# A selective-scan layer on one Trainium2 core: TensorE's half sums of y in front of the fills, GpSimd's first dt*u product of a chunk one place later

## The reference

```python
def step(h, inp):                       # K=4 directions, 192 channels, 16 states
    ul, dl, Bl, Cl = inp
    dA = jnp.exp(dl[..., None] * A)
    h = dA * h + (dl * ul)[..., None] * Bl[:, :, None, :]
    y = jnp.einsum('bkdn,bkn->bkd', h, Cl)
    return (h, y)
```

## Time and profile before

| | |
|---|---|
| Times of three runs | 11091.9, 11092.8, 11114.3 us (median 11092.8) |
| The profiled execution | 11114.1 us, its span 11112.4 us |
| Busy over the span | VectorE 9404 us, TensorE 9796, GpSimd 9035, ScalarE 8690 |
| GpSimd's weighings (L1004) | 3072 of 2383 ns, 7204 us; 358 us idle before them, 278 of it for line 714 |
| VectorE's scans (L779) | 3072 of 2273 to 2333 ns; 518 us idle before them |
| TensorE's granted clock | 0.954 of full speed, mean |

### The profile page before, as it was taken

One profiled execution on the slowest core, in us unless ns is written; L12 is line 12 of the kernel. 1 busy time (PEld: TensorE's weight loads), 2 busy tenths in 40 slices (PEclk: granted clock), 3 DMA queues, 4 the chain that ended last, 5 costly groups with the idle time before them and its releaser, 6 DMA issues. The chain is left out here.

```text
span 11112.4 us, 345302 instructions
## 1 busy us (share of the span) xinstructions
PE 9796.2 (88%) x142892; PEld 6546.6 (59%) x142892; DVE 9404.3 (85%) x5727; ACT 8689.8 (78%) x15618; POOL 9035.1 (81%) x3978
## 2 busy tenths in 40 slices
PE   8978888888888888888888888888888889799999
PEld 5645555555555555555555555555555555588888
DVE  7869999998999999989999998999999999555554
ACT  3468888888888888888888888888888888345453
POOL 1169999999999999999999999999999999534330
PEclk9989999999999999999999999999999999899999
DMA  3356666666666666666666666666666666322220
GB/s 103 108 153 160 167 174 171 161 167 170 174 161 167 177 167 162 168 173 167 159 167 175 166 161 166 175 170 162 172 177 164 159 171 163 84 75 64 70 70 13
DMA packets 547249, 1647.95 MB, mean 148 GB/s; under 512 B 148562, under 2 KB 149362, under 8 KB 542872
## 3 DMA queue, kind: packets, MB, share of 16 engines
q1 hardware_dynamic: 484248, 1416.10, 50.0%
q10 hardware_dynamic: 61440, 209.76, 6.1%
HBM read 1251.98 MB, written 373.29 MB: 146 GB/s over the span
## 5 line engine op out<-in xcount | busy, mean ns | idle before, releaser
L1004 POOL TENSOR_TENSOR HC<-H,crep 128x1024 f32<-128x1024 f32 x3072 | 7203.9, 2383 | 358.0 <-PE psum L714 277.7
L779 DVE TENSOR_TENSOR_SCAN H<-E,car,psum 128x1024 f32<-128x1024 f32 x2304 | 5271.4, 2333 | 344.8 <-PE psum L691 111.2
L880 ACT ACTIVATE E<-dlr,am 128x1024 f32<-128x1024 f32 x3072 | 3497.2, 1145 | 917.2 <-DVE H L779 868.6
L714 PE MATMUL psum<-HC,sely 128*32 128x512 f32 x12288 | 2307.0, 635 | 83.4 <-POOL HC L1004 65.2
L779 DVE TENSOR_TENSOR_SCAN H<-E,psum 128x1024 f32<-128x1024 f32 x768 | 1713.5, 2273 | 173.4 <-PE psum L691 78.1
L691 PE MATMUL psum<-diagp,dluT 128*32 128x128 f32 x49152 | 1630.3, 276 | 256.0 <-DVE H L779 240.8
L691 PE MATMUL psum<-diag,dluT 128*32 128x128 f32 x49152 | 1692.7, 280 | 145.7 <-issue 121.1
L691 PEld LDWEIGHTS psum<-diagp,dluT 128*32 128x32 f32 x49152 | 1387.0, 111 | 681.0 <-DVE H L779 488.9
L691 PEld LDWEIGHTS psum<-diag,dluT 128*32 128x32 f32 x49152 | 1448.2, 112 | 496.0 <-issue 377.3
L862 ACT ACTIVATE sdl<-dluT,blt 128x192 f32<-128x192 f32 x4096 | 1507.5, 444 | 0.0
L680 PE MATMUL psum<-idn,sdl 128*128 128x128 f32 x6144 | 953.2, 305 | 566.2 <-DVE H L779 566.2
(11 more groups left out here) (143 smaller groups left out, 10428.2 us busy)
## 6 DMA issues: line engine op xcount, KB each, us to landing
dlr<-scr_dl SPq DMA_DIRECT2D x3072, 128.0 KB, 4.2
dur<-scr_dlu SPq DMA_DIRECT2D x3072, 128.0 KB, 3.3
crep<-scr_bc SPq DMA_DIRECT2D x512, 256.0 KB, 6.4
crep<-scr_bc SPq DMA_DIRECT2D x1024, 128.0 KB, 3.0
scr_dlu<-dlu SPq DMA_DIRECT2D x256, 384.0 KB, 3.1
scr_yk<-yt ACTq DMA_DIRECT2D x256, 384.0 KB, 3.0
scr_dl<-dlt ACTq DMA_DIRECT2D x128, 384.0 KB, 4.4
scr_dl<-yt ACTq DMA_DIRECT2D x128, 384.0 KB, 4.2
```

What stands on the lines that cost most here:

```text
L714: r = e.matmul(yps[32 * j:32 * j + 32, cols], sely[:], HC[:, (3 * i + j) % NHC, cols], start=g == 0 and k != 0 and not second(m), stop=g = ...
L779: e.tensor_tensor_scan(H[:, un % NH, ::step], decay[:, ::step], drive[:, ::step], init, ALU.mult, ALU.add).then_inc(scan_done)
L880: e.activation(E[:, un % NE, :], dlr[:, slot(m, j), :], ACT.Exp, scale=am[:, ae:ae + 1]).then_inc(exp_done)
L1004: e.tensor_tensor(HC[:, un % NHC, :], H[:, un % NH, :], crep[:, g, :], ALU.mult).then_inc(hc_done)
```

## The change

In TensorE's loop the half sum now comes before `fill(un + 2)`, save at x = 5, where the fill stays first. GpSimd's `delta` of an even step comes at x = 9, behind weighing 8, and no longer at x = 8, behind weighing 7.

```diff
         for un in range(NUNIT + 12):
             n, x = divmod(un, 12)
-            fill(un + FILL_AHEAD)
+            if x == 5:
+                fill(un + FILL_AHEAD)
             if un >= 5 and (un - 5) % 3 < 2 and (un - 5) // 3 < NG * NSTEP:
                 sum_y((un - 5) // 3, (un - 5) % 3)
+            if x != 5:
+                fill(un + FILL_AHEAD)
...
             if n % 2 == 0:
-                if x == 8 and n + 2 < NSTEP:
+                if x == 9 and n + 2 < NSTEP:
                     delta(n + 2)
```

## The result

The changed kernel is slower: median 11138.1 us of six runs (11127.0 to 11150.6), against 11102.7 us for the kernel before in six runs, ratio **1.0031, 95% interval 1.0020 to 1.0042**, +35 us. The forecast was 11150 us and slower. The profiled executions differ by 29.7 us (spans 11112.4 and 11142.1).

A forecast was written before the change was run, and what follows sets the result against it. No engine is full (GpSimd 95%); a loop through several bounds it at 68.8 us a chunk. 68.1 + 0.2 + 1.05 = 69.35, +0.5 over 127 chunks, +65 us: 11150 us, range 10,980 to 11,250.

The forecast's parts named there:

- The bound and the loop: Scan: GpSimd busiest at 95%, but no engine full; time is a loop through several engines, 68.8 us a chunk.
- The cost of the sums in front: TensorE before group 7's sum: idles 2.6 us in one piece, making the next chunk's projection 1.55 us late.
- The clock: TensorE after the 2.6 us idle: clock falls in 3 of 4 chunks, costing 1.4 us each, +1.05 us a chunk.
- The gain at weighing 12: GpSimd's weighing at place 12: group 2's sum comes earlier, offsetting the late projection; start 4471.0 us in both orders.
- Weighing 6: GpSimd's weighing at place 6: its wait, 1.82 us in one chunk, shrinks little, its sum standing behind the late projection.
- two marks: GpSimd's waits: for y sums to fall by half or more, for scans to rise from 63 to over 200 us.
- B: Projection's end to end of weighing at place 7: no separate gain forecast; that weighing ends at 4458.5 in place of 4456.92.
- its -0.7: Whole chunk at full clock: most chunks come near 68.1 us in place of 68.8, -0.7 us a chunk.
- The product's later place: GpSimd's even-step dt*u product: one 2.36 us weighing fills the softplus wait, 112.4 us over all; scan fits by 0.2 us.
- The sum: Whole chunk: 68.1 + 0.2 + 1.05 = 69.35 us against 68.8, +0.5 us a chunk, +65 us.
- the marks set for it: Trace signs: TensorE's HC wait over 400 us, product's softplus wait near nothing, low clock at fill 4, GpSimd's waits shifting.
- The rival from the skill's rule: GpSimd regains its waits, clock falls in 1 chunk of 4 or fewer: 10,960 to 11,070 us, middle 11,020; chance 0.33.

The follow-up runs named there:

- e1: Kernel before with only the dt*u product moved one place later, from x = 8 to x = 9: 11107.0 us, ratio 1.0001 to before.
- e2: Changed kernel with the dt*u product back at x = 8, so only the half sums in front: 11221.3 us, ratio 1.0104 to before.
- e3: Changed kernel with the sums of groups 6 and 7 behind their fills again, product still later: 10989.6 us, ratio 0.9897 to before.

## Why the prediction was right, step by step

**The bound and the loop: right.** The time moved with the chunk's loop, and e1 is its plainest proof: 112 us less waiting of the busiest engine gave nothing.

**The cost of the sums in front: the mechanism right, the size a little off.** Forecast were 2.6 us of idle in one piece; chunk C has 2.90. Forecast was 1.55 us of lateness at full clock. Stretch A without a fall of the clock most often takes 9.70 us in the kernel before and 10.85 in the changed one (the means of such chunks, 10.06 and 11.12, hold a few with other stalls), 1.15 or 1.06 more. Probably I had put the sums and fills one after another with too little overlap; no run separates this.

**The clock: right in sum, in part by luck.** I took 3 chunks of 4 and 1.4 us, 1.05. Measured are 72 of 120 chunks; the usual one with a fall, chunk C among them, takes 12.53 us in A in place of 10.85, so 0.60 x 1.68 = 1.0: I had too many falls at too low a price. Three in four was right for the long wait itself: of the 53 waits of 2.5 us or more ahead of sum 7, 40 are followed by a fall. But I had that wait in most chunks, and 67 of the 120 do not have it; and 23 of the 72 falls lie in chunks with a stall, which the prediction did not know of. That these errors cancel is luck. The Trainium skill (TensorE: Matmul & The Clock Gate, the part on the HAM clock gate) calls the monitor behind the clock free-running, from which I took that a wait of one length may be caught or missed; the new trace agrees: of 46 waits of 2.85 to 2.95 us ahead of sum 7, all in chunks without a stall, 35 are followed by a fall and 11 are not, such as the one at 4800 us:

```profile
4800.46 0.63 PE L714 MATMUL psum<-HC,sely 128*32 128x512 f32 x3 [2.88 <-POOL HC L1007]
...
4801.34 1.92 PE L691 MATMUL psum<-diagp,dluT 128*32 128x128 f32 x62
```

There the fill takes 1.92 us, and A is 10.85 us.

**The gain at weighing 12: right**, 14.07 us to 12.5 in chunk A by the forecast, 13.93 to 12.54 on the mean.

**Weighing 6: wrong in sign.** The prediction said that its wait "shrinks little". It grew from 1.23 to 1.97 us a chunk, since the late projection stands in front of its sum with the clock's fall included, and one fill less does not make up for that. With it two marks failed: GpSimd's wait for sums rose in place of falling by half, and its wait for scans rose to 109 us and not past 200, as weighing 6 took its share of the late scan 7. The loop's length was not touched by this, since both waits end in weighing 7.

**B: its cause not foreseen.** Where sum 0 carries extra products, weighing 6 and not scan 7 set weighing 7, and the missing fill 8 gave time back: B went from 10.04 to 9.41 us in the 12 chunks with the skip alone, from 10.06 to 9.46 in the 48 with the second direction alone, from 11.89 to 10.93 in the 12 with both, and stayed (9.40 and 9.41) in the 48 with neither; 0.40 on the mean. The prediction held this gain only inside its -0.7, since it took chunk A, one of those with neither, for all.

**The product's later place: right, on both counts.** It took the softplus wait away, and e1 and e2 show that it pays only once weighing 12 is released early. That the scan would be there in time held by the narrow margin given; no wait for it shows at weighing 8.

**The sum.** Forecast were 68.1 + 0.2 = 68.3 us for a chunk at full clock and 1.05 for the clock, 69.35, or +0.5. In the changed kernel the 48 chunks without a fall take 68.15 us, and the 72 with one 69.64, so the clock's part is 0.60 x 1.49 = 0.9 and the mean 69.05, or +0.25. Each of the two terms was 0.15 too large. In the kernel before, the 99 chunks without a fall take 68.65 us: at full clock the change gains 0.5 us, and 72 falls in place of 21 take 0.7 back. So the sign hangs on the clock, as the prediction said. Of the marks set for it, TensorE's wait over 400 us, no softplus wait and the low clock at fill 4 came; the two named above did not.

**The rival from the skill's rule** (Perfetto Trace Analysis, Optimization Strategy: find the gaps of the most contended engine and make what they wait for start sooner) points the right way only with a condition. Followed at all eight sums (save the first halves of sums 0 and 4, which stay behind their fills) it gave +0.3%, without sum 7 it gave -1.4%. The one sum that did harm was the one whose making waits for the very engine it is to release.

One thing needs the stalls to be understood: e3 has a fall in A in 37 chunks against 21 before, though TensorE hardly waits for GpSimd in it. Of the 37, 36 lie in its 66 chunks with a stall. The kernel before has such chunks too, 53, but there the stall ends 4.8 us before the end of weighing 23 on the mean, in e3 3.1 us before it, so that the slow stretch behind it more often reaches into A. Why the number of stalls differs from kernel to kernel stays open.

## What to carry to other kernels

Moving a consumer's release ahead of other work on an in-order engine pays only where its own input is ready by then: look place by place for who lags whom, since one of eight places ate the gain of the rest. A wait taken from the busiest engine is worth nothing until the next wait of the same loop goes too, so try edits in pairs. And count a new idle stretch of TensorE twice, for itself and for the clock behind it; but before putting falls of the clock down to it, sort the iterations by what else stood still in front of them.

## What the runs showed of the hardware

TensorE sometimes stands still inside a fill with nothing to wait for that the profile shows, 118.0 us in 68 places of the diagonal fills in the changed kernel, up to 3.8 us each. One of them lies in the chunk after C:

```profile
4450.72 0.38 PE L691 MATMUL psum<-diag,dluT 128*32 128x128 f32 x4 [2.20 <-issue]
...
4452.57 2.85 PE L691 MATMUL psum<-diag,dluT 128*32 128x128 f32 x62
```

The 2.20 us there do what a wait does: the granted clock from 4450.7 to 4454.1 us is 0.52, and the fill behind takes 2.85 us for 62 matmuls in place of 1.92. It is not due to the change: the kernel before has 132.3 us of it in 71 places. In both kernels 61 of these places are in fills 1 and 2 of a chunk.

The traces point to the fetching of instructions. Beside the data queues the profile lists a DMA queue of the kind "instruction" with 1136 packets of 16 KB (packets, MB, share of the 16 DMA engines):

```profile
q8 instruction: 1136, 18.61, 0.7%
```

Every one of TensorE's 75 idle pieces of this kind in the changed kernel's scan, in fills and sums, ends 1.30 to 1.75 us after such a packet has landed; a moment picked at random lies so in fewer than 8 cases of 100. The one above ends 1.48 us after the landing of the packet that started at 4447.93 us. So TensorE most likely stood there for its next instructions. No run tested it.
